# Attention's softmax sum in an audio tower: GpSimd's partial sums laid out with a token's six frames as neighbours

## The reference, cut to what matters

```python
q = (t @ Wq.T + bq).reshape(T, Nw, HEADS, HEAD_DIM)
k = (vd @ Wk.T + bk).reshape(V, Fr, HEADS, HEAD_DIM)
v = (vd @ Wv.T + bv).reshape(V, Fr, HEADS, HEAD_DIM)
logits = jnp.einsum('avhd,bthd->abhvt', k, q) / math.sqrt(HEAD_DIM)
weights = jax.nn.softmax(logits, axis=3)          # over the 12 frames v
attn = jnp.einsum('avhd,abhvt->abhtd', v, weights)
attn = attn.transpose(0, 1, 3, 2, 4).reshape(V, T, Nw, EMBED).mean(axis=0)
o = attn @ Wo.T + bo
```

## Time and profile before

| | |
|---|---|
| median of 3 runs | 2290.06 us (2287.98 to 2292.02) |
| the profiled execution | 2295.13 us |
| its span, first to last instruction | 2293.3 us |
| busy, whole span: PE / DVE / ACT / POOL | 2010.1 / 1628.0 / 1072.4 / 605.2 us |
| attention's loop | about 1070 to 1542 us of the span |

### The profile page before, as it was taken

The page is one execution under the profiler, slowest core; times in us unless marked ns, Lnnn a source line. Parts: engine busy times, 40 slices in busy tenths (PEclk is TensorE's granted clock), DMA queues, the critical chain, the costliest instruction groups (busy, mean ns, idle before and its releaser), DMA issues. The chain is left out here.

```text
span 2293.3 us, 54560 instructions
## 1 busy us (share of the span) xinstructions
PE 2010.1 (88%) x20890; PEld 1782.7 (78%) x20890; DVE 1628.0 (71%) x4095; ACT 1072.4 (47%) x2698; POOL 605.2 (26%) x650
## 2 busy tenths in 40 slices
PE   6699999989636988886999999976999999999998
PEld 5588777778535877884777777765999999999998
DVE  4755556554583755665999999987777777777773
ACT  4433333332344555543666666642444444444443
POOL 0002222220025555511333333333212221221220
PEclk9699999999878999997999999996999999999999
DMA  8100001100211111100000000000000000000000
GB/s 184 42 1 12 11 11 14 14 6 1 76 55 40 42 35 39 39 14 1 3 3 3 3 3 3 3 3 1 8 7 14 7 7 14 7 7 14 7 8 14
DMA packets 80354, 44.50 MB, mean 19 GB/s; under 512 B 45800, under 2 KB 74024, under 8 KB 79752
## 3 DMA queue, kind: packets, MB, share of 16 engines
q1 hardware_dynamic: 74248, 29.53, 5.7%
q0 software_dynamic: 5888, 12.07, 2.0%
HBM read 27.20 MB, written 14.38 MB: 18 GB/s over the span
## 5 line engine op out<-in xcount | busy, mean ns | idle before, releaser
L2127 ACT ACTIVATE w<-banks,b 128x384 f32<-128x384 f32 (+1 forms) x512 | 259.4, 571 | 393.6 <-PE banks L2201 393.6
L2183 PE MATMUL banks<-w,w 128*128 128x128 f32 (+1 forms) x3072 | 364.1, 275 | 0.0
L2183 PEld LDWEIGHTS banks<-w,w 128*128 128x128 f32 (+1 forms) x3072 | 350.4, 189 | 9.1 <-issue 8.7
L1710 PE MATMUL banks<-qT,w 64*64 64x128 f32 (+1 forms) x4608 | 268.1, 269 | 21.7 <-DVE eb L1612 18.5
L1710 PEld LDWEIGHTS banks<-qT,w 64*64 64x64 f32 x4608 | 247.4, 134 | 39.6 <-issue 20.6
L1718 PE MATMUL banks<-eb,w 64*64 64x128 f32 (+1 forms) x4608 | 269.0, 270 | 1.8 <-DVE eb L1612 1.7
L1681 POOL TENSOR_TENSOR t<-eb 128x768 f32<-128x768 f32 x96 | 170.2, 1773 | 309.2 <-ACT eb L1658 306.0
L1718 PEld LDWEIGHTS banks<-eb,w 64*64 64x64 f32 x4608 | 244.0, 133 | 2.5 <-DVE eb L1612 2.5
L2024 DVE SCALAR_TENSOR_TENSOR h<-banks,t_wt,h 128x128 f32 (+3 forms) x672 | 183.7, 343 | 83.2 <-PE banks L2183 79.7
L1237 POOL DMA_INDIRECT xg<-xs,rowu x184 | 181.5, 987 | 128.6 <-DMA xg<-xs,rowu 86.6
L2199 PE MATMUL banks<-t_xh,t_w1h 128*128 128x384 f32 (+1 forms) x512 | 182.5, 357 | 0.0
(11 more groups left out here) (305 smaller groups left out, 4268.4 us busy)
## 6 DMA issues: line engine op xcount, KB each, us to landing
out<-h SPq DMA_DIRECT2D x16, 320.0 KB
xs<-r_xl SPq DMA_DIRECT2D x16, 192.0 KB, 2.9
h<-in_xT SPq DMA_DIRECT2D x4, 750.0 KB, 15.2
h<-in_xT SPq DMA_DIRECT2D x4, 749.0 KB, 18.2
xg<-xs,rowu POOLq DMA_INDIRECT x184
xs<-r_xl SPq DMA_DIRECT2D x16, 128.0 KB
blocks<-NT SPq DMA_DIRECT2D x24, 48.0 KB, 1.9
D<-blocks SPq DMA_DIRECT2D x24, 48.0 KB, 2.0
```

The costliest lines, as they stand in the source:

```text
L1710: last = nc.tensor.matmul(lbanks(n)[place(n, hd), v, 0:wide(n)], k.Kt[half(hd), v, :], qT[half(hd), n // NC % 2, (n % NC) * P:(n % NC) * P ...
L2127: nc.scalar.activation(gb[u % 2][:, f, s * GW:s * GW + NFREE[s]], k.ps[:, order.bank(n), 0:NFREE[s]], ACT.Relu, bias=k.b1_1[:, 2 * e + f:2 ...
L2183: last = nc.tensor.matmul(k.psf[0:n, o:o + P], gb[u % 2][:, f, c * P:c * P + n], k.w2_1[:, 2 * e + f, :], start=(f == 0), stop=(f == 1))
```

## The change

The tile `t1` gets its last two dimensions exchanged, `[P, 2, P, 6]`: for each buffer and token, six neighbouring partial sums. VectorE's reduction L1603 reads each token's six elements side by side, and the whole chunk in one run of 768 (narrow: 636) elements. GpSimd's addition L1681 reads `eb` in the same order as before (a frame, then its tokens), and so writes with a step of six elements (24 bytes) from one token to the next. No instruction, semaphore, wait or buffer is added or removed, and the tile keeps its size.

```diff
-        t1 = sb("t1", [P, 2, 6, P])
+        t1 = sb("t1", [P, 2, P, 6])
@@ VectorE
-                        nc.vector.tensor_reduce(den[:, w % 2, 0:m], t1[:, w % 2, :, 0:m].rearrange("p v t -> p t v"),
-                                                AX_X, ALU.add).then_inc(summed, 1)
+                        nc.vector.tensor_reduce(den[:, w % 2, 0:m], t1[:, w % 2, 0:m, :], AX_X,
+                                                ALU.add).then_inc(summed, 1)
@@ GpSimd
-                    nc.gpsimd.tensor_tensor(t1[:, n % 2, :, 0:m], e[:, 0:6, 0:m], e[:, 6:12, 0:m],
-                                            ALU.add).then_inc(tree, 1)
+                    nc.gpsimd.tensor_tensor(t1[:, n % 2, 0:m, :].rearrange("p t v -> p v t"), e[:, 0:6, 0:m],
+                                            e[:, 6:12, 0:m], ALU.add).then_inc(tree, 1)
```

## The result

The changed kernel takes 2270.92 us (median of 4 runs, 2266.61 to 2274.96), the kernel before 2289.11 in the same comparison (2287.98 to 2292.02). The ratio on record is 0.9914, with a 95% interval from 0.9897 to 0.9931 (the two medians alone divide to 0.9921): faster by 0.9%. The forecast was 2273.

What follows compares the result with a forecast made beforehand. VectorE was taken to set the attention loop's pace, TensorE close behind. 88 chunks gain 12.6 us (0.86 per six) and the last 8 gain 4.4, together 17.0: 2273 us from the median 2290.06, range 2262 to 2304.

Steps and rivals of the forecast that it cites:

- Part one: VectorE's sum L1603 reads neighbours: 1.507 us falls to 0.953 wide, 1.256 to 0.82 narrow, together 51.4 us.
- the last rival: At the sum L1603, distance is not what makes it slow; it stays near 1.5 us, 2290 or slower; 8%.
- Part two: GpSimd's addition L1681 writes with a step of 24 bytes and still takes 1.82 us.
- The rivals at 2.46 and 2.90 us: GpSimd's scattered write L1681 costs 0.64 us more (2284 to 2289, 13%) or 1.09 more (2306, slower, 19%).
- Part three: In the attention loop, TensorE and a loop of waits through GpSimd hold six chunks at 27.9 us, from 28.75.
- the rival at 2239: VectorE's saving in the attention loop arrives whole, 51 us less, with TensorE's stretches elastic; 4%.
- TensorE's 26.94 us: TensorE's six iterations in the attention loop, without waits, sum to 26.94 us; as the only hold, 2259 us.
- the loop through GpSimd: VectorE's scaling waits behind GpSimd's addition, so two iterations last at least 9.37, 9.09, 8.39 or 7.85 us.
- ScalarE's delay behind the narrow chunk: ScalarE's logarithm, exponential, normalization and copy delay the next turn by some 0.3 us; without it 2269.
- VectorE still without idle time: Sign in the next profile that the forecast is wrong: VectorE still shows no idle time.
- the line above it: Expected sign: the scaling L1612's mean rises above 1.858 us, or VectorE idles before it until ScalarE's `rd`.

Runs made afterwards that it cites:

- The two halves of the change, tried alone: Against the kernel before, VectorE reads neighbours in the old layout: 2269.86 us; against the changed kernel, VectorE reads 512 bytes apart: 2294.42 us.
- the run with one input: Against the changed kernel, the scaling L1612 replaced by a reduction reading the same elements of `eb` alone, weights unscaled: 2262.29 us.
- three frames: Against the changed kernel, GpSimd adds three frames to three in place of six to six, sums wrong: 2261.41 us, ratio 0.9873.

## Why the prediction was right

**Part one** forecast 0.953 and 0.82 us for the sum; 0.940 and 0.802 were measured, 52.6 us in all against 51.4. Borrowing the price from a reduction of the same element count elsewhere in the trace was enough. The second support was weaker than it looked: the maximum L1607, taken as confirming the rate of neighbours, itself reads each token's 12 logits 512 bytes apart, but in PSUM. By itself it could as well have spoken for the last rival, that distance costs nothing. The two halves of the change, tried alone, settle it for SBUF.

**Part two** took the mild end, 1.82 us, and 1.835 was measured. The rivals at 2.46 and 2.90 us did not occur. The Trainium skill's rule in "GPSIMD Engine Reference", section "Performance pitfalls for Q7 kernels", on operands read with a long step does not carry over to a write of this shape: in an addition that takes 2.05 ns an element, a write every 24 bytes cost 0.02 ns an element more. Nor does the Trainium skill's rule of "Advanced Engine Details and Errata", section "Memory Cachelines", that full speed takes at least two hits on a 16-byte line, show in it. One figure of that rival was off: 0.64 us over 768 elements is 0.83 ns each, 1.9 times what L645's read adds, not 1.5.

**Part three** is what made the number right. Without it the forecast would have been the rival at 2239. TensorE's 26.94 us appear as 27.01 wherever nothing else holds, and the loop through GpSimd answers in both directions as its bounds say. In the changed kernel itself it binds where forecast: the two waits of TensorE's products, ahead of the narrow chunk's iteration and ahead of the turn, were to be 0.50 and 0.15 us (9.37 less 8.87, 13.33 less 13.18), and are 0.52 and about 0.1. The first of them stood there before the change too (0.51), so all of the gain is in the iteration behind it.

**The term that was off** is ScalarE's delay behind the narrow chunk, put at 0.3 us. The turn was to start about 7.0 us behind the first product of the narrow chunk's iteration; it started at 6.78 (1203.85 to 1210.63). That is 0.05 behind the end of ScalarE's copy, but only 0.08 later than TensorE's products alone allow: the last of them started 0.28 before the turn, where 0.20 is the distance in the run with one input. ScalarE's instructions overlap where I had added them up: from the logarithm's start to the normalization's is 0.56 us (0.65 in the sum), from there to the copy's 1.16 (1.25). Six chunks came to 27.66 in place of 27.9. Over 88 chunks that is 16.6 us gained (from the first scaling to the 89th: 422.67 before, 406.08 after) for 12.6 forecast. In the tail it was the other way: 2.8 us over the seven steps from the 89th scaling to the last (30.47 to 27.70), where 0.55 a step would be 3.9, as some of these scalings meet GpSimd too (the third takes 2.02 us). The two errors cancel only in part, 19.4 us against 17.0, and of the 22.5 us by which the profiled executions differ in span the remaining 3.1 lie ahead of the loop.

That the median came within 2.1 us of the forecast is therefore partly luck. The loop gained 2.4 us more than forecast, and the stretch ahead of it, which the change does not touch, differs by up to 11 us between the profiled runs.

One of the signs of being wrong did come true: "VectorE still without idle time". It is recorded as busy for 27.66 of 27.66 us. The sign contradicted the line above it, which allowed longer scalings in place of idle time, and that is what happened: the scaling's mean rose to 2.181 us, and idle time appears once the additions are short or the blocking is gone (14.6 us before the scaling with three frames, 30.4 with one input). The sign was badly chosen, as a blocked instruction counts as busy.

## What to carry to other kernels

A gain on the engine that sets the pace is worth only the distance to the next hold; add up the runner-up's instructions over a whole period of the pattern, and each loop of waits over the iterations that it spans, before believing the saving. An engine with half of its time idle can still hold the pace if its instruction shuts another engine out, and then starting it earlier in pieces can beat making it do less. A busy share of 100% may hide standing still: compare an instruction's mean with its shortest.

## What the runs showed of the hardware

- VectorE reads single float32 elements in SBUF at 512 bytes' distance in 1.9 ns each, and neighbours in 1.04 (differences of the 768- and 636-element forms over 132 elements): 1.507 us against 0.940 for 768.
- VectorE's maximum reads single elements 512 bytes apart in PSUM in 1.04 ns each (1.742 us for 1536, 1.466 for 1272), the rate that neighbours have in SBUF.
- GpSimd's addition of two operands writes 24 bytes apart as fast as side by side: 1.835 and 1.817 us.
- VectorE's two-input scaling in SBUF and GpSimd's addition shut each other out, in both directions. The second to start ends later by what the first has left, less 0.12 to 0.14 us. I had expected only the direction that the trace of before showed; the other cost GpSimd 1.5 us in a 0.74 us instruction.
